# Another order in the passage from a Mamba block to a ternary feed-forward block, and TensorE's loops written out

## The chip, the cores and the metric

The kernel runs on 1 core of a Trainium2 chip. The metric is the device time of one execution in microseconds (us). One execution was also profiled; its rows are the source of all that is read below.

## What is computed

Two sequences of 2048 tokens with 512 features pass one layer. The reference, cut to what matters:

```python
# attention part: a Mamba-2 block (8 heads of 128, state 64, chunks of 64)
zxbcdt = u @ W_in.T
xBC = silu(conv4(xBC) + conv_b);  dt = softplus(dt + dt_bias)
y = ssd(x, dt, -exp(A_log), B, C) + x * D
yg = y * silu(z)
yn = yg * rsqrt(mean(yg * yg) + 1e-5) * norm_w
x1 = layernorm(u + yn @ W_out.T)
# feed-forward part: ternary weights
w_q = clip(round(w / mean|w|), -1, 1) * mean|w|        # for W_up, W_gate, W_down
hidden = silu(x1 @ w_up.T) * (x1 @ w_gate.T)           # 2048 wide
out = layernorm(x1 + hidden @ w_down.T)
```

## The kernel before

The work is cut into 8 blocks of 512 tokens (`NB` = 8, 4 chunks `C` of 128). Each engine runs a program of its own, written out by hand, and they meet through counting semaphores: `wait_ge(sem, n)` holds an engine's whole queue until the count is reached. SyncE (SP) issues all transfers, in its program's order.

*Attention part.* `step(n, par)` does block n in four head pairs p. TensorE projects x and z tiles (`head_tile`, line 931, 12 matmuls of 512 columns each into one of three ring banks), turns x (line 984), makes the states (`states`, line 994) and the outputs (`outputs`, lines 1004 and 1012), and in pair 1 the four output chunks of the block before (`chunk_out`, line 960). VectorE does the convolution (1793), the mask (`within`, which writes `seg`, 1891), the state updates (1905, the last of which writes `carry`), `skip` (1913), and for each chunk `residual` (1928 to 1936) and `normalise` (1940). GpSimd takes the root for `rstd` (1584). The outputs of a block's last head pair come in the next block's pair 0. For each chunk SP loads the token rows (`load_utok`, line 620) once the residual two chunks before is done, and stores the normalised rows (`store_x1`, line 624). `run_steps` calls blocks 0 and 1, then a hardware loop (line 524, two turns of two blocks) for 2 to 5, then 6 and 7.

*Feed-forward part.* `x1` of a block is split into a high and a low half-precision part in seven pieces (j = 0 to 6, factors and sums of a Strassen-like scheme of seven products): ScalarE writes the high part (`x_high`, 1402), VectorE the low (`x_low`, 1968), SP transposes both (`turn_x`, DMA transposes, line 695). Each hidden group q (eight to a block) takes products 1 to 7 (line 1126, 8 matmuls of 256 columns each). Products 1, 6 and 7 go to one bank in turn; ScalarE reads the bank after each (`chain_read`, 1504) into `s1`, `u2` and `u3`, and VectorE adds (`summed`, 2143) to get `c11`, `c12`, `c21`, `c22`. Then come ScalarE's tanh (1513), VectorE's `hidden` (2151), GpSimd's `hidden` (1704), ScalarE's high part (1521), VectorE's `hidden_low` (2158), and TensorE's `down` (1146). `ffn_steps` calls step(-1), 0 and 1, then a hardware loop (line 537, two turns of two steps) for 2 to 5, then 6 and 7. TensorE is one of five engines with these two loops.

*The passage.* Block 7 of the attention part already splits and transposes block 0 for the feed-forward part, in its pairs 1 and 2. After block 7, TensorE does product 1 of (block 0, q = 0), then the last head pair's outputs between the other products. `ffn_step(-1)` (q = 1 to 7) still has to finish block 7's output chunks: `last_squares` (1167) sums the squares, VectorE writes `ms` (2228), GpSimd the root `rms` (1747), `last_chunk(c, half)` (1183) makes the chunks in the two `p_down` banks, and VectorE takes `residual(7, c)` in steps q = 2, 3, 4 and 6. `last_chunk(2, 0)` in step 3 needs the bank of chunk 0 and so waits for `residual(7, 0)`. The function that calls TensorE's blocks in the attention part is

```python
def run_steps(eng, step):
    step(0, 0)
    step(1, 1)
    with eng.Fori(0, QN // 2) as i:
        step(i * 2 + Q0, 0)
        step(i * 2 + (Q0 + 1), 1)
    step(NB - 2, 0)
    step(NB - 1, 1)
```

Of the kernel before, what the change touches and what calls it, by code (L numbers as in the profile page):

```python
# [32 lines left out]
NB = 8  # L33
# [126 lines left out]
def build(nc, a, out):  # L160
    with ExitStack() as ctx:
# [156 lines left out]
        turn_free = sem("turn_free")  # L318
# [260 lines left out]
        def _(sp):  # L579
# [134 lines left out]
            def step(n, par):  # L714
                for p in range(4):
# [24 lines left out]
                    if p == 2:  # L740
                        if not is_at(n, 0):
                            if is_at(n, NB - 1):
                                for j in range(4):
                                    turn_x(0, 0, j)
                            store_x1(n - 1, 0)
                            load_utok(n - 1, 2)
                            if is_at(n, NB - 1):
                                turn_x(0, 0, 4)
                            store_x1(n - 1, 1)
                            load_utok(n - 1, 3)  # L750
                            store_x1(n - 1, 2)
# [132 lines left out]
        def _(pe):  # L884
# [231 lines left out]
            run_steps(pe, step)  # L1116
# [81 lines left out]
            product(0, 0, 0, 1, True)  # L1198
            pe.wait_ge(s1_ok, 1)
            product(0, 0, 0, 6, False)  # L1200
            pe.wait_ge(turn_free, turn_use(NB, "x01") + 1)
            product(0, 0, 0, 5, True)
# [69 lines left out]
            ffn_steps(pe, ffn_step)  # L1272

        @block.scalar
        def _(act):
# [258 lines left out]
            gated(NB, 0, 1)  # L1534
            act.wait_ge(scales_ok, 3)
            gated(NB, 1, 0)
            gated(NB, 1, 1)

            def ffn_step(t, par):
                n, own = t + 1, 1 - par  # L1540
                for q in range(1 if is_at(t, -1) else 0, NQ):
                    before, earlier = pair_at(t, par, q, 1), pair_at(t, par, q, 2)
                    if before:
                        m, its, k = before
                        wait(act, act_ok, 2 * (m * NQ + k) - 1)
# [3 lines left out]
                    if has_up(t):  # L1549
                        wait(act, act_ok, 2 * (n * NQ + q) - 2)  # L1550
                        chain_read(n, q, s1, prod[1], s1_ok, c11_ok)
                    for j in splits_at(t, q):
                        x_high(t + 2, par, j)
                    if before:
                        hidden_tanh(m, k, True, not has_up(t))
                        hidden_tanh(m, k, False, not has_up(t))
# [8 lines left out]
        def _(pool):  # L1565
# [167 lines left out]
            def ffn_step(t, par):  # L1733
                for q in range(1 if is_at(t, -1) else 0, NQ):
# [7 lines left out]
                    if before:  # L1742
                        m, its, k = before
                        hidden(m, k, True)
                        if is_at(t, -1) and q == 2:
                            pool.wait_ge(ms_ok, 1)
                            pool.tensor_tensor(rms[:, :], ms[:, :], exponent[:, :], ALU.pow).then_inc(rms_ok, 1)
                        hidden(m, k, False)
# [8 lines left out]
        def _(dve):  # L1757
# [277 lines left out]
            def step(n, par):  # L2035
                first, end = is_at(n, 0), is_at(n, NB)
                for p in range(2 if first else 0, 4):
# [51 lines left out]
                    if p == 1 and is_at(n, NB - 1):  # L2089
# [6 lines left out]
                        residual(n - 1, 0, ring[ring_bank("chunk", 0)])  # L2096
                        x_low(0, 0, 2)
                        x_low(0, 0, 3)
                        normalise(n - 1, 0)
                        residual(n - 1, 1, ring[ring_bank("chunk", 1)])  # L2100
                        x_sum(2)
                        x_low(0, 0, 4)
                        normalise(n - 1, 1)
                        residual(n - 1, 2, ring[ring_bank("chunk", 2)])
                        x_sum(3)
                        normalise(n - 1, 2)
# [204 lines left out]
```

## Time and profile before

| | |
|---|---|
| time, median of 3 runs | 1399.34 us (1397.88 to 1401.0) |
| the profiled execution's own time | 1399.36 us |
| its span, first to last instruction | 1397.6 us |
| TensorE matmuls busy | 1348.4 us (96%) |
| VectorE busy | 1069.8 us (77%) |
| ScalarE busy | 787.5 us (56%) |
| GpSimd busy | 649.8 us (46%) |
| mean granted TensorE clock | 0.992 |
| mean busy share of the DMA queue q1 | 35.6% |

In the rows PE is TensorE's matmuls and PEld its weight loads, DVE is VectorE, ACT ScalarE, POOL GpSimd, SPq SyncE's queue. `[2.94 <-DVE carry L1905]` says that the engine had been idle for 2.94 us and that VectorE's instruction of line 1905, which writes `carry`, released it; "issue" says that nothing in the profile held it. Ends of matmuls are modelled. Buffers are reused under other names in the feed-forward part: there `ring`, `p_seg` and `p_st` hold the chain of products 1, 6 and 7, `p_turn` products 3 and 5, `cum_g` is `s1` and `u2`, `grow` is `u3`, `xdt` holds `c21` and `c22`, `rows` the token rows and the residual.

### The profile page before, as it was taken

The numbers are of one execution on the slowest core, as the hardware profiler recorded it, in microseconds if no ns is written. First come the engines' busy times: TensorE is split into PE (matmuls) and PEld (weight loads), VectorE is DVE, ScalarE is ACT, GpSimd is POOL, SyncE is SP. The second block draws the span as 40 slices with busy tenths as digits, with TensorE's granted clock in tenths as the row PEclk, the third lists the DMA queues.
The fourth block names the chain that finished last, engine by engine and source line by source line (L and its number), as shares of the span: only waits on it lengthen the run. The fifth ranks groups of instructions, "written<-read, shape, count | busy, mean of one in ns | idle before, by whom it ended". The sixth has DMA issues, their size and how long they took to land.

```text
span 1397.6 us, 27164 instructions
## 1 busy us (share of the span) xinstructions
PE 1348.4 (96%) x9446; PEld 872.8 (62%) x9446; DVE 1069.8 (77%) x1848; ACT 787.5 (56%) x1561; POOL 649.8 (46%) x628
## 2 busy tenths in 40 slices
PE   8899999999999999999989999999999999999998
PEld 4455555555555555555546677777777767777774
DVE  6887887886887878868686777777777767777775
ACT  6686574773855837738556555454454545444441
POOL 0574264573663746625346434344343434444331
PEclk9899999999999999999999999999999999999999
DMA  7436333262443542523647342213232222222102
GB/s 246 158 129 224 128 106 99 84 174 79 106 122 98 152 109 80 160 85 95 158 141 225 69 136 47 83 47 67 59 72 69 71 62 58 80 61 54 31 24 68
DMA packets 162798, 143.87 MB, mean 103 GB/s; under 512 B 101344, under 2 KB 123232, under 8 KB 161504
## 3 DMA queue, kind: packets, MB, share of 16 engines
q1 hardware_dynamic: 162656, 142.05, 35.6%
q8 instruction: 80, 1.31, 0.4%
q14 instruction: 62, 0.51, 0.1%
HBM read 99.93 MB, written 27.39 MB: 91 GB/s over the span
## 4 chain that ended last, share of the span: by engine, by line
PE 55%; issue 14%; DVE 13%; ACT 9%; POOL 6%; DMA 1%; SPq 1%; ACTq 0%; POOLq 0%; DVEq 0%
PE ring L1146 15%; PE p_turn L1126 7%; PE p_y L1126 7%; PE p_st L1126 5%; PE p_seg L1126 5%; PE ring L931 5%; PE ring L960 4%; DVE acc L1793 3%; ACT p_seg L1363 2%; ACT xdt L1354 2%; DVE seg L1891 2%; PE p_y L1004 1%; POOL sq_sum L1621 1%; PE p_y L1012 1%; DVE st L1905 1%
## 5 line engine op out<-in xcount | busy, mean ns | idle before, releaser
L931 PE MATMUL ring<-u_split,weights 128*128 128x512 f16 x1620 | 377.6, 383 | 2.3 <-DVE x_ch L1798 2.0
L931 PEld LDWEIGHTS ring<-u_split,weights 128*128 128x128 f16 x1620 | 155.5, 99 | 173.8 <-issue 9.9
L1704 POOL TENSOR_TENSOR xdt<-xdt 128x512 f32<-128x512 f32 x64 | 100.7, 1573 | 340.9 <-DVE xdt L2151 340.9
L1793 DVE SCALAR_TENSOR_TENSOR acc<-ring,taps,acc 128x511 f32<-128x511 f32 (+2 forms) x192 | 143.7, 749 | 4.5
L960 PE MATMUL ring<-w_out,raw 128*128 128x512 f16 x672 | 147.1, 379 | 0.0
L1354 ACT ACTIVATE xdt<-p_turn,dts 128x128 f32<-128x128 f32 x256 | 73.0, 376 | 73.7 <-PE p_turn L984 73.7
L960 PEld LDWEIGHTS ring<-w_out,raw 128*128 128x128 f16 x672 | 65.8, 99 | 77.7
L1613 POOL TENSOR_TENSOR raw<-yg,raw 128x512 f16<-128x512 f32 x64 | 78.8, 1231 | 76.0 <-ACT raw L1384 75.3
L1608 POOL TENSOR_TENSOR yg<-y_ch,z_ch 128x512 f32<-128x512 f32 x64 | 81.6, 1275 | 46.3 <-DVE y_ch L1913 46.3
L1307 ACT ACTIVATE ring<-acc 128x512 f32<-128x512 f32 x64 | 38.5, 602 | 87.1 <-DVE acc L1793 86.6
L1363 ACT ACTIVATE p_seg<-cum_rows,cum 128x128 f32<-128x128 f32 x256 | 80.8, 388 | 10.1 <-DVE seg L1891 10.1
L1004 PE MATMUL p_y<-seg,xdt 128*128 128x128 f32 x512 | 70.6, 281 | 15.0 <-DVE seg L1891 14.7
L1584 POOL TENSOR_TENSOR rstd<-var_e,exponent 128x1 f32<-128x1 f32 x32 | 20.1, 627 | 130.0 <-DVE var_e L1936 130.0
L1004 PEld LDWEIGHTS p_y<-seg,xdt 128*128 128x128 f32 x512 | 64.3, 191 | 25.3 <-DVE seg L1891 20.9
L1621 POOL TENSOR_TENSOR sq_sum<-sq_sum,sq 128x512 f32<-128x512 f32 x56 | 71.2, 1272 | 0.0
L1513 ACT ACTIVATE cum_g<-c_dec,tanh_scale 128x512 f32<-128x512 f32 x32 | 23.1, 722 | 73.4 <-DVE b_dec L2143 73.4
L1513 ACT ACTIVATE cum_g<-b_dec,tanh_scale 128x512 f32<-128x512 f32 x32 | 23.1, 722 | 71.5 <-DVE c_dec L2143 70.9
L1891 DVE TENSOR_TENSOR seg<-p_seg,cb_mask 128x512 f32<-128x512 f32 x64 | 43.9, 686 | 21.3 <-ACT p_seg L1367 21.3
L1513 ACT ACTIVATE grow<-xdt,tanh_scale 128x512 f32<-128x512 f32 x64 | 45.9, 717 | 19.6 <-DVE xdt L2143 19.0
L1798 DVE SCALAR_TENSOR_TENSOR x_ch<-ring,acc 128x512 f32<-128x512 f32 x64 | 44.1, 689 | 15.0 <-ACT ring L1307 14.0
L2143 DVE TENSOR_TENSOR xdt<-grow,p_turn 128x512 f32<-128x512 f32 x64 | 44.0, 687 | 13.9 <-ACT grow L1504 8.2
L2143 DVE TENSOR_TENSOR c_dec<-cum_g,p_turn 128x512 f32<-128x512 f32 x32 | 22.0, 689 | 39.4 <-PE p_turn L1126 39.4
(392 smaller groups left out, 3306.5 us busy)
## 6 DMA issues: line engine op xcount, KB each, us to landing
cum_rows<-cum_dram SPq DMA_DIRECT2D x64, 256.0 KB, 4.2
quant<-in_w_ffn SPq DMA_DIRECT2D x24, 512.0 KB, 4.4
quant<-in_w_ffn SPq DMA_DIRECT2D x48, 256.0 KB, 4.1
cum_g<-cum_dram SPq DMA_DIRECT2D x64, 128.0 KB, 4.5
rows<-in_u_tok SPq DMA_DIRECT2D x32, 256.0 KB, 4.3
x_dram<-rows SPq DMA_DIRECT2D x32, 256.0 KB, 2.0
tern_ug<-quant SPq DMA_DIRECT2D x32, 256.0 KB, 3.4
u_raw<-in_u_t SPq DMA_DIRECT2D x7, 1024.0 KB, 8.1
```

Source lines behind the costliest of these rows:

```text
L931: mm = pe.matmul(bank_k[:, :], w_in[:, ws, k, col:col + P], us[:, par, k * T:(k + 1) * T], start=(i == 0), stop=(i == 3 * KD - 1))
L960: mm = pe.matmul(ring[b][:, :], ys[:, h, c * P:(c + 1) * P], w_out[:, ws, h, :], start=(h == 0 and ys is y_hi and ws == 0), stop=(h == H - ...
L1004: pe.matmul(p_y[q][:, c * P:(c + 1) * P], xdt[:, q, c, :], seg[:, q, c, :], start=(c == 0), stop=False, skip_group_check=True)
L1126: mm = pe.matmul(bank_j[:, w * 256:(w + 1) * 256], factor(weight, w, k, q), xs[par][i][:, k, :], start=(first and w == 0 and k == 0 and xs ...
L1146: mm = pe.matmul(p_down[c % 2][:, :], hidden_tile(par, m, low)[:, c * P:(c + 1) * P], t_down(m), start=(e == 0 and m == 0 and not low), st ...
L1354: ins = act.activation(xdt[:, q, c, :], p_turn[:, c * P:(c + 1) * P], ACT.Copy, scale=dts[:, owner, c, h:h + 1])
L1363: ins = act.activation(p_seg[:, c * P:(c + 1) * P], cum_b[:, (2 * p - 2 + q) % 4, c, :], ACT.Relu, bias=cum[:, owner, h, c:c + 1], scale=-1.0)
L1513: act.activation(th[second], up, ACT.Tanh, scale=tanh_scale[:, 0:1]).then_inc(tanh_ok, 1)
L1608: pool.tensor_tensor(yg[:, q, :], y_ch[:, q, :], z_ch[:, k % 4, :], ALU.mult).then_inc(yg_ok, 1)
L1621: pool.tensor_tensor(sq_sum[:, :], sq_sum[:, :], sq[:, q, :], ALU.add).then_inc(sqsum_ok, 1)
L1704: pool.tensor_tensor(tile_[:, 1, :, :], tile_[:, 0, :, :], tile_[:, 1, :, :], ALU.mult).then_inc(hid_ok, 1)
L1793: dve.scalar_tensor_tensor(acc[:, buf, k + 1:T], own[:, 0:T - 1 - k], taps[:, h, 2 - k:3 - k], acc[:, buf, k + 1:T], ALU.mult, ALU.add).th ...
```

## The change

The order of steps changes in four engines' programs, in the passage only; and TensorE's two loops are replaced by calls for each block, while the other engines keep theirs.

- SP, block 7: stores and row loads of block 6's chunks come earlier among the transposes.
- TensorE: product 5 of (0, 0) moves ahead of product 6.
- ScalarE: the reads of product 7 of (0, 0) and of product 1 of (0, 1) move ahead of `gated(8, 1, 0)` and `gated(8, 1, 1)`; in `ffn_step(-1)` the first tanh moves ahead of `x_high`.
- GpSimd, step (-1), q = 2: `rms` comes ahead of `hidden`.
- VectorE: in block 7 another order of `residual`, `normalise`, `x_low` and `x_sum`; in `ffn_step(-1)` the first `hidden` ahead of `x_low`, and `residual(7, 0)` ahead of `c12` instead of at the step's end.

```diff
@@ SP, block NB - 1, p == 2
-                                for j in range(4):
+                                for j in range(2):
                                     turn_x(0, 0, j)
                             store_x1(n - 1, 0)
                             load_utok(n - 1, 2)
                             if is_at(n, NB - 1):
-                                turn_x(0, 0, 4)
+                                for j in range(2, 4):
+                                    turn_x(0, 0, j)
                             store_x1(n - 1, 1)
                             load_utok(n - 1, 3)
+                            if is_at(n, NB - 1):
+                                turn_x(0, 0, 4)
                             store_x1(n - 1, 2)
                             store_x1(n - 1, 3)
@@ TensorE
-            run_steps(pe, step)
+            for n in range(NB):
+                step(n, n % 2)
...
             product(0, 0, 0, 1, True)
+            pe.wait_ge(turn_free, turn_use(NB, "x01") + 1)
+            product(0, 0, 0, 5, True)
             pe.wait_ge(s1_ok, 1)
             product(0, 0, 0, 6, False)
-            pe.wait_ge(turn_free, turn_use(NB, "x01") + 1)
-            product(0, 0, 0, 5, True)
...
-            ffn_steps(pe, ffn_step)
+            ffn_step(-1, 1)
+            for t in range(NB):
+                ffn_step(t, t % 2)
@@ ScalarE
             gated(NB, 0, 1)
+            chain_read(0, 0, u3, prod[7], u3_ok, c21_ok)
             act.wait_ge(scales_ok, 3)
             gated(NB, 1, 0)
+            chain_read(0, 1, s1, prod[1], s1_ok, c11_ok)
             gated(NB, 1, 1)
...
+                    if before and not (is_at(t, -1) and q == 1):
                         wait(act, act_ok, 2 * (m * NQ + k) - 1)
                         chain_read(m, k, u3, prod[7], u3_ok, c21_ok)
                     if earlier:
                         hidden_high(*earlier, False)
-                    if has_up(t):
+                    if has_up(t) and not (is_at(t, -1) and q == 1):
                         wait(act, act_ok, 2 * (n * NQ + q) - 2)
                         chain_read(n, q, s1, prod[1], s1_ok, c11_ok)
-                    for j in splits_at(t, q):
-                        x_high(t + 2, par, j)
+                    if not is_at(t, -1):
+                        for j in splits_at(t, q):
+                            x_high(t + 2, par, j)
                     if before:
                         hidden_tanh(m, k, True, not has_up(t))
+                    if is_at(t, -1):
+                        for j in splits_at(t, q):
+                            x_high(t + 2, par, j)
+                    if before:
                         hidden_tanh(m, k, False, not has_up(t))
@@ GpSimd
-                        hidden(m, k, True)
                         if is_at(t, -1) and q == 2:
                             pool.wait_ge(ms_ok, 1)
                             pool.tensor_tensor(rms[:, :], ms[:, :], exponent[:, :], ALU.pow).then_inc(rms_ok, 1)
+                        hidden(m, k, True)
                         hidden(m, k, False)
@@ VectorE, block NB - 1, p == 1
                         residual(n - 1, 0, ring[ring_bank("chunk", 0)])
+                        normalise(n - 1, 0)
+                        residual(n - 1, 1, ring[ring_bank("chunk", 1)])
                         x_low(0, 0, 2)
                         x_low(0, 0, 3)
-                        normalise(n - 1, 0)
-                        residual(n - 1, 1, ring[ring_bank("chunk", 1)])
+                        normalise(n - 1, 1)
                         x_sum(2)
+                        residual(n - 1, 2, ring[ring_bank("chunk", 2)])
                         x_low(0, 0, 4)
-                        normalise(n - 1, 1)
-                        residual(n - 1, 2, ring[ring_bank("chunk", 2)])
+                        normalise(n - 1, 2)
                         x_sum(3)
-                        normalise(n - 1, 2)
                         residual(n - 1, 3, ring[ring_bank("chunk", 3)])
                         normalise(n - 1, 3)
@@ VectorE, feed-forward step
+                    if attention_rest(t, q) == 0:
+                        residual(NB - 1, 0, p_down[0])
                     if before:
                         summed(m, k, "c12", u2, u2_ok, 5, ALU.add)
                     if has_up(t):
                         summed(n, q, "c11", s1, s1_ok, 2, ALU.add)
+                    if is_at(t, -1) and before:
+                        hidden(m, k, True)
                     for j in splits_at(t, q):
                         x_low(t + 2, par, j)
...
                     if before:
-                        hidden(m, k, True)
+                        if not is_at(t, -1):
+                            hidden(m, k, True)
                         hidden(m, k, False)
...
-                    if attention_rest(t, q) is not None:
+                    if attention_rest(t, q):
                         residual(NB - 1, attention_rest(t, q), p_down[attention_rest(t, q) % 2])
```

## Rows read from the trace of the kernel before

**Rows 1.** Busy time by stretches: window, us, engines (instructions), PEclk, DMA, GB/s.

```profile
715.85:719.26 3.41, 3.41 (x10) 1.20 (x9) 3.34 (x6) 2.31 (x6) 2.91 (x4) 0.50 0.30 79
749.00:825.00 76.00, 70.52 (x570) 53.52 (x567) 54.53 (x92) 38.24 (x65) 41.10 (x33) 1.00 0.50 148
825.00:1128.00 303.00, 303.00 (x2282) 223.01 (x2280) 228.70 (x359) 152.45 (x252) 126.21 (x95) 1.00 0.26 66
1128.00:1140.00 12.00, 9.13 (x70) 6.63 (x69) 5.01 (x8) 3.54 (x7) 2.86 (x2) 1.00 0.44 139
```

**Rows 2.** TensorE, 749 to 825 us: start, us, engine, line, operation, idle, releaser.

```profile
751.31 1.05 PE L1126 MATMUL ring<-b_tok,weights 128*128 128x256 f16 x8 [0.69 <-ACT cum_g L1504]
...
756.04 1.05 PE L1126 MATMUL ring<-u_raw,weights 128*128 128x256 f16 x8
...
762.06 1.05 PE L1126 MATMUL p_turn<-c_ch,weights 128*128 128x256 f16 x8 [1.37 <-DVE xdt L2143]
...
781.35 2.76 PE L1183 MATMUL ring<-w_out,raw 128*128 128x512 f16 x12 [1.55 <-DVE rows L1928]
...
819.81 1.05 PE L1126 MATMUL p_turn<-c_ch,cum_rows 128*128 128x256 f16 x8 [1.44 <-DVE xdt L2143]
820.70 1.04 PE L1126 MATMUL p_seg<-b_tok,weights 128*128 128x256 f16 x8
```

**Rows 3.** Timeline of TensorE in block 7.

```profile
714.86 1.09 PE L994 MATMUL p_st<-xdt,b_dec 128*64 128x128 f32 x16 [2.94 <-DVE carry L1905]
715.89 4.42 PE L931 MATMUL ring<-u_split,weights 128*128 128x512 f16 x12
...
721.78 1.16 PE L1004 MATMUL p_y<-seg,xdt 128*128 128x128 f32 x8 [0.58 <-DVE seg L1891]
```

**Rows 4.** Timeline of SyncE's queue and VectorE in block 7.

```profile
703.69 0.43 SPq L620 DMA_DIRECT2D rows<-in_u_tok  x1
...
706.52 0.75 DVE L1928 SCALAR_TENSOR_TENSOR rows<-ring,rms,rows 128x512 f32<-128x512 f32 x1 [2.93 <-DMA rows<-in_u_tok]
...
710.05 0.75 DVE L1928 SCALAR_TENSOR_TENSOR rows<-ring,rms,rows 128x512 f32<-128x512 f32 x1
...
721.04 0.68 DVE L1891 TENSOR_TENSOR seg<-p_seg,cb_mask 128x512 f32<-128x512 f32 x1
```

**Rows 5.** Timeline of ScalarE, VectorE and GpSimd in the passage.

```profile
760.63 0.58 ACT L1504 ACTIVATE grow<-ring 128x512 f32<-128x512 f32 x1
...
771.16 0.15 DVE L2228 TENSOR_SCALAR ms<-ring 128x4 f32<-128x4 f32 x1
...
775.24 0.69 DVE L2143 TENSOR_TENSOR b_dec<-cum_g,p_turn 128x512 f32<-128x512 f32 x1 [3.27 <-PE p_turn L1126]
...
779.42 1.02 POOL L1747 TENSOR_TENSOR rms<-ms,exponent 128x4 f32<-128x4 f32 x1
...
780.54 0.75 DVE L1928 SCALAR_TENSOR_TENSOR rows<-ring,rms,rows 128x512 f32<-128x512 f32 x1 [2.21 <-issue]
...
817.95 0.99 DVE L2158 SCALAR_TENSOR_TENSOR z_ch<-xdt,hid_scale,z_ch 128x512 f16<-128x512 f32 x1
```

**Rows 6.** The loop lines 524 and 537: ns min/median/max, first to last start.

```profile
L524 PEldq COMPARE_BRANCH  x2: 83/2503/4923, 371.6 to 557.5; - x2
...
L537 PEldq COMPARE_BRANCH  x2: 83/1790/3497, 1128.5 to 1284.8; - x2
```

**Rows 7.** Timelines of TensorE and VectorE behind the jumps back of both loops.

```profile
376.81 0.65 PE L984 MATMUL p_turn<-ident,x_ch 128*128 128x128 f32 x4 [1.80 <-issue]
...
379.58 1.41 DVE L1913 SCALAR_TENSOR_TENSOR y_ch<-x_ch,d_skip,p_y 128x512 f32<-128x512 f32 x2 [4.20 <-issue]
...
388.46 1.16 PE L1004 MATMUL p_y<-seg,xdt 128*128 128x128 f32 x8 [0.77 <-DVE seg L1891]
...
1134.18 0.69 DVE L2143 TENSOR_TENSOR xdt<-grow,p_turn 128x512 f32<-128x512 f32 x1 [2.77 <-ACT grow L1504]
...
1137.26 1.04 PE L1126 MATMUL p_turn<-c_ch,cum_rows 128*128 128x256 f16 x8
```

## The prediction

> **What bounds the kernel now.** I read four views: the busy time by stretches, the timelines around the idle spots of TensorE, the list of waits, and the rows of the two loop lines.
>
> The stretches [rows 1] show the bound. In the feed-forward part, 825 to 1128 us, TensorE is busy 303.00 of 303.00 us: nothing that another engine does there costs time, and whatever TensorE gains earlier is kept to the end. From 749 to 825 it is busy 70.52 of 76.00 us, and from 1128 to 1140, around the jump back of the feed-forward loop, 9.13 of 12.00. Those, with the stretch before 725, hold what this change can win or lose. TensorE's shown ends are modelled: a product of eight 256-column matmuls shows 1.05 us, and the next starts 0.89 after it [rows 2]. So a stall costs TensorE the shown idle time plus about 0.17 us (1.05 - 0.89 = 0.16).
>
> **Part 1, the row loads and the vector order of block 7 (before 725 us).** `states(7, 2)` stands 2.94 us behind VectorE's carry update; the matmuls after it then take 4.42 us for a tile whose like takes 2.76 [rows 2, 3], since TensorE is granted 0.50 of its clock from 715.85 to 719.26 [rows 1]; and the second half of `outputs` waits 0.58 more for `seg` [rows 3]. What VectorE does before: `residual(6, 2)` waits 2.93 us for its token rows, whose load is issued at 703.69 behind four transposes, and `residual(6, 3)` starts at 710.05, its load issued after residual 2; the second `seg` of block 7 follows at 721.04 [rows 4].
>
> The diff issues store 0 and load 2 after two transposed splits instead of four. Both need only residual 0 and normalise 0, which on VectorE now come before splits 2 and 3. Load 3 takes the place at 703.69 that load 2 had. Then residual 2 is limited by TensorE's chunk, not by a load, and residual 3 can start when rows issued at 703.69 land: 706.52 by the row of today's load 2. That is 710.05 - 706.52 = 3.53 us earlier. What is left between residual 3 and the second `seg` (710.05 to 721.04) keeps its order, so `seg` ends 3.5 us earlier and so does TensorE's wait on it. The 2.94 stall goes: the carry that released `states` at 714.86 is then there at 711.3, and TensorE comes to it at 714.86 - 2.94 = 711.92. The half clock goes with it. In exchange the wait before the second half of `outputs` grows from 0.58 to about 1.5 us, so not all of 2.94 + (4.42 - 2.76) + 0.58 = 5.2 comes back. I take **3.5**. Bounds: 0 if a transpose lands later because a load is now ahead of it and splits 2 to 4 stand before residual 3 as late as today, 5.2 if VectorE also gets shorter.
>
> **Part 2, TensorE and ScalarE at the start of the feed-forward part.** Product 6 waits 0.69 us for ScalarE's read of product 1 [rows 2]. Product 5, whose only wait is for ScalarE's `x_dt`, the same that `states` asked for before it, is put between: 0.89 us of work covers 0.69 + 0.17. **0.9**, bounds 0.7 and 0.9.
>
> Product 3 of step q = 1 waits 1.37 us for `c22`, which waits for ScalarE's read of product 7 at 760.63 [rows 2, 5]. That read stands behind two `gated` groups that wait for GpSimd, though product 7 starts at 756.04 and ends near 757. The diff puts it ahead of them: the read then ends near 757, `c22` and `c21` follow `c11` on VectorE near 758 to 759, and TensorE comes to product 3 at 759.6 in the new time. The read of product 1 of q = 1 moves up too, between the two `gated`; it asks for a product that ends at about 759, when the second `gated` would start anyway. **1.5** (1.37 + 0.17). Lower bound 0.5: the next thing TensorE asks for is the last `y_low` of GpSimd, now due within 0.2 us of the time when TensorE comes to it, so a microsecond may come back as a wait there.
>
> **Part 3, the residual of the last block and `rms`.** `last_chunk(2, 0)` waits 1.55 us for residual 0 at 780.54, which waits for `rms`. `ms` is written at 771.16 but GpSimd makes `rms` at 779.42, behind the `hidden` of the same step [rows 2, 5]. The diff makes `rms` first, so it is there near 772.3 in today's time, and puts the residual before `c12` on VectorE, in an idle stretch of 3.27 us. Its four short instructions should end by 774.5; `c12` starts only at 775.24, when product 3 is done [rows 5], so nothing is pushed. **1.7** (1.55 + 0.17), bounds 0.7 (if `c12` is pushed and product 5 waits) and 1.7.
>
> The earlier `hidden` in the splits' steps lets GpSimd start 0.6 us sooner per step. Only at q = 7 does TensorE wait there: 1.44 us for `c22` behind `hidden_low` at 817.95 [rows 2, 5]. VectorE is contiguous before it: `c11`, split, `hidden`, `hidden`, residual 3, `hidden_low`, and the sum stays the same in any order. I take **0.1**, bounds 0 and 1.6. The moved `x_high` and splits have microseconds of slack, since their transposes feed products that come later: 0.
>
> **Part 4, the loops of TensorE.** The rows of the two loop lines hold two branches each on TensorE: 83 ns where it falls through, 4923 and 3497 ns where it jumps back [rows 6]. After the jumps TensorE shows idle 1.80 us and 12.00 - 9.13 = 2.87 us [rows 1, 7]; its queued matmuls cover the rest. Written out, those jumps are gone. But VectorE, ScalarE, GpSimd and SyncE keep theirs.
>
> Feed-forward jump: TensorE would reach product 3 at 1137.26 - 2.87 - 2 x 0.17 = 1134.05. That product needs `c22`, which VectorE starts at 1134.18 after its own jump and ends at 1134.87 [rows 7]. TensorE waits 0.9 there. 3.2 - 0.9 = **2.3**; bounds 1.5 and 3.2 (if VectorE's jump too gets shorter once TensorE's fetch is gone).
>
> Attention jump: VectorE is idle 4.20 us until 379.58, and then works without a gap up to the `seg` that TensorE waits for before 388.46 (0.77 us) [rows 7]. If TensorE comes 1.80 us earlier it waits that much longer at 388.46. **0**; bounds 0 and 2.0, the latter if VectorE's own 4.20 shrinks.
>
> **A rule against the trace.** The rows say 4923 and 3497 ns for the two jumps back and 83 ns for falling through [rows 6]. The Trainium skill, Advanced Engine Details and Errata, section Control Flow Timing, gives about 108 ns for a compare-and-branch. By that figure, four branches cost 0.4 us and part 4 would be worth nothing that can be measured; the sum by it would be 1391.7. This trace does not agree with it for a jump that is taken. The skill's page Runtime: NRT & Kernel Launch, Instruction fetch mechanics, says instead that a taken branch out of the fetched window forces a fetch before execution can go on, which is the side the rows are on.
>
> **The sum.** 3.5 + 0.9 + 1.5 + 1.7 + 0.1 + 2.3 + 0 = 10.0 us. The profiled execution took 1399.36 us with a span of 1397.6, so 1.8 us lie around the span; the median of the three runs shown is 1399.34, the same. 1399.4 - 10.0 = **1389.4 us**, 0.7% less.
>
> **Rivals.**
> - *The fetch stalls of the other engines shrink too.* After TensorE's jump VectorE stalls 4.20 us, longer than the feed-forward jump's 2.77 [rows 7]; if TensorE's fetch was in its way, the attention jump gives up to 2.0 and the feed-forward jump 0.9 more: 1386.5 us. Against it: no row shows that the two stalls have a common cause, and VectorE's jump stays. 0.15.
> - *Part of the stalls turns into new waits* (the `y_low` of part 2, a split behind a later transpose in part 1, or the jumps give nothing because the idle time comes from elsewhere, 10.0 - 2.3). Gains of 3 to 8 us, centre 1393. 0.16.
> - *No effect*: the gaps are taken up by VectorE, whose work is unchanged. It is the releaser in most rows of [rows 2, 3]. For it to hold, part 1 must give nothing and parts 2 and 3 must return at q = 7, where TensorE waits for VectorE. Within 2.8 us of before: 1398. 0.04.
> - *Slower: the written-out stream is fed late.* The loops' turns are 557.5 - 371.6 = 186 and 1284.8 - 1128.5 = 156 us long [rows 6], so 684 us are written out. If a refill comes late it costs what the jump cost, 3.5 to 4.9 us [rows 6]; from the third late refill on, 3 x 4.9 = 14.7 outweighs 10.0 and the kernel gets slower: about 1404 us. Against it: 825 to 1128 runs straight ahead, without a jump back, and shows no such idle in 303 us [rows 1]. 0.04.
> - The forecast as it stands, 8 to 12 us gained: 0.61.
>
> **Numbers.** Prediction 1389.4; its own case spans 1387.4 to 1391.4. The range takes in the first rival and most of the second: 1386.0 to 1394.5. About 0.2% (2.8 us) is what a measurement of this kernel can tell from no change. Faster 0.92, same 0.04, slower 0.04.
>
> **What would show it.** Part 1: no idle before `states` at block 7's third head pair, no half clock near 715, load 3 issued before transposed split 4, the wait before the second `outputs` half at about 1.5 us. Part 2: product 5 between 1 and 6; no wait of product 3 at q = 1. Part 3: `rms` about 1 us after `ms`, `last_chunk(2, 0)` without idle; the wait at q = 7 still there. Part 4: no idle of TensorE right at the two former jumps, but longer waits on `seg` (2.5 instead of 0.77) and of about 0.7 on `c22` behind it; VectorE's own idle there unchanged. The prediction is wrong if residual 3 does not start some 3.5 us sooner relative to block 7, if the last `y_low` holds TensorE for more than 1 us, or if the other engines' jumps change length.

## The result and the profile after

The changed kernel takes 1388.67 us (median of 5 runs, 1387.74 to 1391.2) against 1398.60 for the kernel before (5 runs on the same chip, 1396.11 to 1401.0): ratio 0.9935, 95% interval 0.9921 to 0.9949, or 9.9 us less by the medians. The profiled execution took 1387.94 us with a span of 1386.2. The forecast was 1389.4.

Where the time came from is read in the same way for every run below: the start of the same matmul is compared in two traces. TensorE's first matmul is set to zero in both, and the difference is how far the stream has come ahead of the kernel before. Taken at twelve matmuls it gives the gain of each stage (us, minus is earlier). Each row is one profiled execution:

| kernel | start to 374 | attention jump | to 710 | block 7 | prod. 6 | prod. 3, q=1 | `y_low` | `last_chunk(2,0)` | q=4 | q=7 | 825 to 1128 | feed-forward jump |
|---|---|---|---|---|---|---|---|---|---|---|---|---|
| changed kernel | -2.19 | -0.53 | -0.08 | -4.14 | -0.87 | -1.54 | +0.30 | -1.72 | +0.61 | +0.63 | 0.00 | -1.87 |
| e1_order_only | -1.37 | -1.10 | -0.13 | -3.18 | -0.86 | -1.54 | +0.31 | -1.72 | +0.61 | +0.63 | 0.00 | -0.58 |
| e2_loops_only | -1.87 | -0.64 | -0.15 | -1.03 | 0.00 | 0.00 | 0.00 | 0.00 | -0.01 | +0.02 | 0.00 | -2.08 |
| e3_hidden_last | +0.16 | -1.11 | -0.15 | -4.14 | -0.87 | -1.54 | +0.31 | -1.72 | 0.00 | 0.00 | 0.00 | -2.05 |
| e4_all_straight | -1.97 | -2.56 | -1.32 | -4.14 | -0.86 | -1.54 | +0.31 | -1.72 | +0.61 | +0.63 | +1.41 | -3.21 |
| e5_block7_only | -2.38 | -1.05 | -0.18 | -3.31 | -0.01 | 0.00 | 0.00 | 0.00 | -0.01 | -0.01 | 0.00 | +0.27 |
| e6_block7_vector | -1.45 | -0.09 | +0.01 | +4.19 | 0.00 | +0.01 | 0.00 | 0.00 | -0.01 | 0.00 | 0.00 | +0.43 |
| e8_best | -1.36 | -2.57 | -1.43 | -4.15 | -0.87 | -1.54 | +0.31 | -1.72 | 0.00 | 0.00 | 0.00 | -3.21 |
| e9_residual_later | -1.36 | -2.56 | -1.33 | -4.14 | -0.86 | -1.54 | +0.31 | -1.72 | -0.01 | +0.05 | +0.75 | -3.21 |
| e10_reads_back | +0.15 | +0.08 | -0.08 | -4.14 | -0.87 | +0.37 | 0.00 | -1.72 | +0.61 | +0.93 | +1.10 | -2.10 |
| e11_rms_back | -0.44 | -0.93 | -0.11 | -4.15 | -0.86 | -1.54 | +0.30 | -0.16 | +0.61 | +0.62 | 0.00 | -2.05 |
| e12_fetch_on | -0.40 | -0.94 | -0.07 | -3.60 | -0.86 | -1.54 | +0.32 | -1.72 | +0.61 | +0.96 | +1.07 | -2.10 |
| e13_fetch_off | -0.33 | -0.40 | +0.03 | -1.88 | -0.87 | -1.54 | +0.31 | -1.72 | +0.61 | +0.62 | 0.00 | -2.28 |

The first column moves by up to 2.5 us between kernels whose code there is the same, so it is the chance of one execution; the second does by 1.2. From product 6 to q = 7 equal code gives equal numbers to some 0.02 us, but for two cases told below: e10 and e12, where lower clock begins in the column q = 7, and block 7, where TensorE's instruction packets play a part. The feed-forward jump is less exact: kernels that keep the loop there show -0.58, +0.27 and +0.43. Without the first column the changed kernel has 9.2 us, which agrees with the times within their interval.

The passage in the changed kernel, TensorE's timeline (the rows that answer to [rows 2, 3]):

```profile
709.03 1.09 PE L997 MATMUL p_st<-xdt,b_dec 128*64 128x128 f32 x16
710.06 2.76 PE L934 MATMUL ring<-u_split,weights 128*128 128x512 f16 x12
...
714.82 1.16 PE L1007 MATMUL p_y<-seg,xdt 128*128 128x128 f32 x8 [1.11 <-DVE seg L1905]
...
779.51 2.75 PE L1187 MATMUL ring<-w_out,raw 128*128 128x512 f16 x12
...
783.67 1.05 PE L1130 MATMUL p_turn<-c_ch,weights 128*128 128x256 f16 x8 [0.53 <-DVE xdt L2157]
...
810.26 1.05 PE L1130 MATMUL p_turn<-c_ch,cum_rows 128*128 128x256 f16 x8 [2.06 <-DVE xdt L2157]
...
1125.84 1.05 PE L1130 MATMUL p_turn<-c_ch,cum_rows 128*128 128x256 f16 x8 [1.17 <-DVE xdt L2157]
```

`states` has no wait, its next tile takes 2.76 again, the wait on the second `seg` grew from 0.58 to 1.11, and the waits of [rows 2] are gone save the last, which went from 1.44 to 2.06. New is 0.53 at q = 4 (with 0.17 more at the product behind it, not shown). Busy time by stretches, those of [rows 1] in the new time (window, us, engines with instructions, PEclk, DMA, GB/s):

```profile
711.71:715.12 3.41, 2.30 (x16) 1.65 (x14) 3.27 (x10) 3.30 (x6) 1.62 (x3) 1.00 0.56 175
741.50:815.47 73.97, 70.73 (x575) 54.13 (x575) 60.59 (x92) 39.27 (x67) 42.43 (x32) 1.00 0.51 155
815.47:1118.46 302.99, 302.99 (x2282) 223.00 (x2280) 229.41 (x359) 151.87 (x252) 126.14 (x95) 1.00 0.26 66
1118.46:1129.50 11.04, 9.88 (x74) 7.04 (x73) 5.71 (x9) 4.45 (x8) 3.38 (x3) 1.00 0.50 147
```

VectorE is busy 60.59 us in the passage, where it was 54.53 [rows 1], with the same 92 instructions. That is the lead to the new wait.

### The profile page after: what moved, and what is told of

Its sections match the earlier page's. It is cut to its first block, busy times and chain, and to the rows that moved or that the text cites. A ratio compares the mean times of both kernels' runs of the same rounds, so it can differ in the third digit from the quotient of the medians.

```text
span 1386.2 us, 26970 instructions
## 1 busy us (share of the span) xinstructions
PE 1344.7 (97%) x9446; PEld 872.4 (63%) x9446; DVE 1075.3 (78%) x1848; ACT 786.7 (57%) x1561; POOL 650.7 (47%) x628
## 3 DMA queue, kind: packets, MB, share of 16 engines
q8 instruction: 75, 1.23, 0.4%
## 4 chain that ended last, share of the span: by engine, by line
PE 44%; issue 22%; DVE 14%; POOL 9%; ACT 9%; DMA 1%; POOLq 0%; ACTq 0%; SPq 0%; DVEq 0%
PE ring L1150 11%; PE p_turn L1130 5%; PE p_y L1130 5%; PE ring L934 5%; PE ring L963 5%; PE p_st L1130 4%; PE p_seg L1130 4%; DVE acc L1807 3%; ACT p_seg L1369 3%; ACT xdt L1360 2%; DVE seg L1905 1%; PE p_y L1007 1%; POOL sq_sum L1635 1%; PE p_y L1015 1%; DVE st L1919 1%
```

## The experiments

Times are medians. Each ratio is against the kernel before as it was measured beside them on the same chip: 1397.87 us for e1 to e4, 1397.84 for e5, e6, e8 and e9, 1397.55 for e10 and e11, 1397.79 for e12 and e13. Beside the changed kernel it was 1398.60, so a difference of 1 us between the median of a run and the 1388.67 of the changed kernel shows nothing by itself; small terms are read from the table.

### Which half does it: the order or the loops

**e1_order_only** is the changed kernel with TensorE's loops kept, **e2_loops_only** the kernel before with only them written out.

```diff
e1:  -            for n in range(NB):
     -                step(n, n % 2)
     +            run_steps(pe, step)
e2:  the reverse, in the kernel before
     (both also for ffn_steps)
```

> The changed kernel with TensorE's two loops put back: only the order of steps in the passage differs from before. If the parts add up as the two traces read (order 9.9 us up to the end of the wait at q = 7 less the losses there, jumps 2.5), this gains about 6.7 us over before, so 1391.9 against 1398.6, and TensorE shows idle 1.80 us behind the attention jump and 2.87 in the stretch of the feed-forward jump again. Rival: the straight code also helps in the passage (a refill that came late there), then the order alone gains under 5 us.

> The kernel before with TensorE's two loops written out and nothing else changed. Theory, that the jump's stall on TensorE goes and the wait for VectorE's own jump takes part of its place: gain 2.5 us (0.6 in the attention part, 1.9 in the feed-forward part), TensorE idle about 1.2 us at each of the two places, and VectorE's idle behind the attention jump 2.8 us instead of 4.2. Rival, that a compare-and-branch costs some 0.1 us and the idle time comes from elsewhere: no gain. Rival, that VectorE's shorter stall in the attention part was chance: gain 1.9, VectorE idle 4.2 again.

e1: 1393.92 us (12 runs), ratio 0.9976 (0.9963 to 0.999). e2: 1395.53 (11 runs), 0.9977 (0.9965 to 0.999). In the table the two halves add up in block 7 and the passage to the changed kernel: block 7 3.18 + 1.03 = 4.21 against 4.14. But 1.03 us of block 7 comes from the loops, though TensorE's code there is the same. By the times e1's theory (6.7 us) failed: its median is 4.0 us under the kernel before, 3.4 by the ratio, where its trace has 5.8 from block 7 to q = 7. The two medians together give 6.3 us of the 9.9. The traced execution of e1 took 1390.45 us, and its runs go from 1389.82 (mean granted clock 0.996) to 1400.59 (0.991): the four at 0.991 took 1395.96 to 1400.59, the two at 0.995 and 0.996 1392.29 and 1389.82. So part of the gap goes with the clock. Why e1 is at the lower clock more often is not explained.

### The new waits at q = 4 and q = 7

**e3_hidden_last**: the changed kernel with VectorE's first `hidden` and ScalarE's first tanh back behind the splits.

```diff
-                    if is_at(t, -1) and before:
-                        hidden(m, k, True)
                     for j in splits_at(t, q):
                         x_low(t + 2, par, j)
...
                     if before:
-                        if not is_at(t, -1):
-                            hidden(m, k, True)
+                        hidden(m, k, True)
                         hidden(m, k, False)
     (on ScalarE x_high stands ahead of the first tanh again)
```

> The changed kernel with one part undone: in the steps -1, VectorE's first hidden stands behind the splits again, and ScalarE's first tanh behind its split. Theory: GpSimd's hidden product, started sooner, runs beside VectorE's splits and its normalise and stretches them (2.36 us for two splits instead of 1.28), which gave TensorE 0.53 us of wait at q = 4 and 2.06 instead of 1.44 at q = 7. Then the split pair takes 1.28 us again, the wait at q = 4 is under 0.1, that at q = 7 about 1.4, and the kernel is 1.2 us faster than the changed one. Rival: the residuals that come earlier, not the hidden, load VectorE; then both waits stay and the time too.

1387.56 us, ratio 0.9923 (0.991 to 0.9936). The wait at q = 4 is gone and the one at q = 7 is 1.44 again: 1.24 us by the trace. The medians are 1.1 us apart, and the intervals of the two ratios overlap, so it is the trace that shows the size. The mechanism stands in the timelines of the changed kernel, VectorE and then GpSimd:

```profile
776.32 0.69 DVE L2165 SCALAR_TENSOR_TENSOR xdt<-grow,xdt 128x512 f32<-128x512 f32 x1
776.92 2.36 DVE L1982 TENSOR_TENSOR u_raw<-quant,u_raw 128x512 f16<-128x512 f32 x2
...
786.58 0.69 DVE L1982 TENSOR_TENSOR u_raw<-quant,u_raw 128x512 f16<-128x512 f32 x1
787.19 1.50 DVE L1954 TENSOR_SCALAR rows<-rows,mv,rstd 128x512 f32<-128x512 f32 x1
...
805.17 1.76 DVE L2165 SCALAR_TENSOR_TENSOR b_dec<-cum_g,b_dec 128x512 f32<-128x512 f32 x1
```

```profile
777.08 1.65 POOL L1718 TENSOR_TENSOR xdt<-xdt 128x512 f32<-128x512 f32 x1 [1.52 <-DVE xdt L2165]
...
786.75 1.65 POOL L1718 TENSOR_TENSOR xdt<-xdt 128x512 f32<-128x512 f32 x1 [3.56 <-DVE xdt L2165]
...
804.73 1.65 POOL L1718 TENSOR_TENSOR xdt<-xdt 128x512 f32<-128x512 f32 x1 [2.66 <-DVE xdt L2165]
```

The early `hidden` lets GpSimd start in the middle of VectorE's splits. In this trace an instruction of VectorE with both inputs in SBUF that starts while GpSimd's runs ends only behind it: 804.73 + 1.65 = 806.38, and VectorE's `hidden`, 0.69 alone, ends at 806.93. Of the instructions with one SBUF input only `normalise` is held, at 1.50 instead of 0.54; the statistics of 789.98, beside GpSimd's of 789.36, take their 0.69. It works the other way too: from the passage on GpSimd's `hidden` takes 1.65 to 1.71 us in all 52 cases where it starts inside such an instruction of VectorE, and 1.27 in nearly all of the other 76. In e3 the two splits are done before GpSimd starts, and take 1.29:

```profile
778.01 1.29 DVE L1977 TENSOR_TENSOR u_raw<-quant,u_raw 128x512 f16<-128x512 f32 x2
779.22 0.54 DVE L1949 TENSOR_SCALAR rows<-rows,mv,rstd 128x512 f32<-128x512 f32 x1
779.67 0.68 DVE L2160 SCALAR_TENSOR_TENSOR xdt<-grow,xdt 128x512 f32<-128x512 f32 x1
780.28 0.69 DVE L2160 SCALAR_TENSOR_TENSOR c_dec<-cum_g,c_dec 128x512 f32<-128x512 f32 x1
780.88 0.75 DVE L1937 SCALAR_TENSOR_TENSOR rows<-ring,rms,rows 128x512 f32<-128x512 f32 x1
```

The `hidden` of 780.28 began ahead of GpSimd's at 780.44 and was not held; the residual of 780.88, which reads `ring` in PSUM, was not either. The Trainium skill, SBUF — State Buffer, section "SBUF: two separate sides", says that VectorE (with two SBUF inputs, or in a two-port mode) and GpSimd share one pair of ports, that it is an exclusive lock, and that whoever starts first keeps it for the whole instruction. The trace agrees: VectorE lost 0.96 to 1.08 us each time in the rows above.

### What the other engines' loops cost

**e4_all_straight**: the changed kernel with the loops of all five engines written out.

```diff
 def run_steps(eng, step):
-            step(0, 0)
-            step(1, 1)
-            with eng.Fori(0, QN // 2) as i:
-                step(i * 2 + Q0, 0)
-                step(i * 2 + (Q0 + 1), 1)
-            step(NB - 2, 0)
-            step(NB - 1, 1)
+            for n in range(NB):
+                step(n, n % 2)
     (the same in ffn_steps; two conditions that knew the loop's blocks by
      their type now go by the block's number)
```

> The changed kernel with the loops of all five engines written out, not only TensorE's. Theory: what is left at the two jumps are the jumps of VectorE and ScalarE. Then TensorE's 1.23 us idle at 375.8 and 1.17 at 1124.6 go, each with about 0.17 more, and VectorE's idle of 2.8 and 3.2 us there too: 2.5 to 3 us faster than the changed kernel. Rival: more code for five engines means more refills on the shared queues, some of them late: no gain, or idle spots at new places.

1384.92 us, ratio 0.9907 (0.9893 to 0.992). The attention jump now gives 2.56 us and the feed-forward jump 3.21, with no idle time of TensorE behind either; 1.24 us more come before 710, where TensorE's waits on `seg` from 392 us on sum to 4.0 us instead of 5.0. Against that, 1.41 us are lost behind the wait at q = 7. Stretches of e4 behind that wait, same columns as above:

```profile
807.40:809.20 1.80, 1.80 (x16) 1.48 (x15) 1.80 (x4) 0.72 (x1) 0.00 (x0) 0.83 1.01 378
809.20:812.40 3.20, 3.20 (x19) 2.29 (x18) 3.14 (x4) 1.78 (x3) 1.50 (x1) 0.56 0.41 154
```

The granted clock falls towards its lower level (1.2 GHz) after the 2.06 us of idle time. The changed kernel has the same 2.06 and stays at 1.00. Of seven profiles with that wait, three (e4, e10, e12) show the fall, at 1.40 us each (in e10 and e12 0.3 of it stands in the column q = 7 of the table); of the seven where it is at most 1.50, none shows a fall there.

### Block 7: the row loads, the vector order, and what neither did

**e5_block7_only** is the kernel before with the block 7 edits of SP and VectorE, **e6_block7_vector** with VectorE's alone.

```diff
e5 and e6, VectorE, block 7:
                         residual(n - 1, 0, ring[ring_bank("chunk", 0)])
+                        normalise(n - 1, 0)
+                        residual(n - 1, 1, ring[ring_bank("chunk", 1)])
                         x_low(0, 0, 2)
                         x_low(0, 0, 3)
     ...
e5 alone, SP:
-                                for j in range(4):
+                                for j in range(2):
                                     turn_x(0, 0, j)
     ...
```

> The kernel before with the order of block 7 alone (the row load of block 3 issued ahead of the transposing load on SP, residual 2 and 3 moved on VectorE), every loop as before. Theory: TensorE's stream comes ahead by 2.9 to 3.2 us in block 7 (the loops-only run, which has none of it, already came ahead 1.0 us there, so about 1 us of the 4.1 us seen is not this edit's), so the time falls by about 3 us, ratio 0.998. Rival: the gain of block 7 is the transposes' pace of one execution; then the time stays within 1 us of before.

> The same, but with VectorE's order alone; SP issues its loads as before. If the seg wait of block 7 was VectorE standing behind residual 2 for its row load (2.93 us), the order on VectorE alone removes it: as much gain as with both edits (about 3 us) as long as the rows of block 3 still land before they are read. If the row load is what counts, residual 3 now waits for it, and less than 1.5 us is gained.

e5: 1394.80 us (12 runs), ratio 0.9981 (0.997 to 0.9993), block 7 3.31 us earlier. e6: 1401.83 (12 runs), 1.0028 (1.0015 to 1.0041), slower. The theory (3 us gained) was wrong; its alternative had the mechanism, residual 3 waiting for its load, but not the loss. VectorE, e6:

```profile
705.12 0.75 DVE L1928 SCALAR_TENSOR_TENSOR rows<-ring,rms,rows 128x512 f32<-128x512 f32 x1 [6.17 <-DMA rows<-in_u_tok]
...
712.70 0.75 DVE L1928 SCALAR_TENSOR_TENSOR rows<-ring,rms,rows 128x512 f32<-128x512 f32 x1 [3.52 <-DMA rows<-in_u_tok]
```

With the loads where they were, residual 2 waits 6.17 us, now with the split of j = 4 behind it, whose transpose stands on SP ahead of the load of residual 3 (issued at 709.49, before it was 707.34); residual 3 waits 3.52 more, and TensorE 7.13 for the carry. The vector order is worth something only with the loads. Whether the loads alone would do it was not run.

In e1 and e5, with the loops kept, residual 3 waits 1.99 and 1.94 us for its rows; in the changed kernel they are there (landed at 702.68) and it waits 1.12 for TensorE's chunk. VectorE, e5, then changed kernel:

```profile
703.12 0.75 DVE L1931 SCALAR_TENSOR_TENSOR rows<-ring,rms,rows 128x512 f32<-128x512 f32 x1 [1.94 <-DMA rows<-in_u_tok]
```

```profile
703.09 0.75 DVE L1942 SCALAR_TENSOR_TENSOR rows<-ring,rms,rows 128x512 f32<-128x512 f32 x1 [1.12 <-PE ring L963]
```

With the shift of the stream taken out (3.61 and 2.81 us), residual 3 starts 3.32 us sooner in e5 and 4.15 in the changed kernel, and block 7 gives 3.31 and 4.14: its start sets the gain of block 7.

The 1.03 us of e2 in block 7 has another source. In the four traces with TensorE's loops kept, four transposes of block 7 take 6.44 to 6.66 us on SP's queue; in the eight of e1 to e11 and the changed kernel with them written out, 5.45 to 5.55. Kernel before, then changed kernel, each in the window of those four transposes (DMA queues: packets, MB, share):

```profile
689.38 6.50 SPq L695 DMA_TRANSPOSE xs_more<-u_raw  x4
...
q1 hardware_dynamic: 1766, 1.54, 115.0%
q8 instruction: 1, 0.02, 0.8%
```

```profile
686.56 5.46 SPq L695 DMA_TRANSPOSE xs_more<-u_raw  x4
...
q1 hardware_dynamic: 1855, 1.57, 103.5%
```

A 16 KB packet of instructions (0.88 us long, at 693.41) falls among them before and not after. There are 80 of them before and 75 after, and 75 still in e4 and e8, where the other engines' loops are written out too: so they are TensorE's. Two runs move them on purpose. **e12_fetch_on** and **e13_fetch_off** make eight and four head tiles of block 2 of twice as many, half as wide matmuls:

```diff
-                        mm = pe.matmul(bank_k[:, :], w_in[:, ws, k, col:col + P], us[:, par, k * T:(k + 1) * T], ...)
+                        for at in range(0, T, T // parts):
+                            mm = pe.matmul(bank_k[:, at:at + T // parts], w_in[:, ws, k, col:col + P],
+                                           us[:, par, k * T + at:k * T + at + T // parts], ...)
...
+    parts = 2 if is_at(n, 2) and kind == "x" and h < 8 else 1      (h < 4 in e13)
```

In these two the second half's first matmul restarts the bank, so part of the sums of the split tiles is dropped and the results are not those of the layer; everything else is as in the changed kernel.

> The changed kernel, with the twelve 512-column matmuls of each of eight head tiles of block 2 made as twice as many 256-column matmuls: 96 more matmuls with 96 more weight loads, whose columns are the same in number. TensorE's instruction stream gets 192 instructions longer far ahead of block 7, so each later 16 KB piece of it is fetched some 19 us earlier in the program: the one at 709.1 us comes near 690, within the four transposes of block 7 (686.56 to 692.02), as it did in the kernel before (693.4, within 689.38 to 695.88). Theory: the packet of about 1 us holds up the transposes, which take 6.4 to 6.7 us again instead of 5.5, and TensorE's stream gains 3.2 us in block 7 instead of 4.1: about 1 us slower than the changed kernel. Rival: where the fetch falls has nothing to do with it; 5.5 us and 4.1 us stay.

> The same with four head tiles of block 2 split, 96 instructions more. The fetch comes near 699 us, outside the four transposes. Theory: they stay at 5.5 us and block 7 keeps its 4.1 us; the time is that of the changed kernel plus what the 48 added matmuls cost by themselves (nothing, if two of 256 columns take as long as one of 512). Rival (any split of the tiles slows block 7): 6.5 us here as well.

e12: 1390.50 us, ratio 0.9946 (0.9927 to 0.9965). The packet starts at 687.80 (1.74 us long) and the first transpose takes 2.63 us instead of 1.5; the four take 6.54 us, and block 7 gives 3.60 instead of 4.14:

```profile
687.98 6.54 SPq L695 DMA_TRANSPOSE xs_more<-u_raw  x4
```

e13: 1392.48 us, 0.9956 (0.9943 to 0.997). The four stay at 5.50, but the packet, at 698.46, meets the next pair of transposes, which takes 3.36 us (2.57 in the changed kernel, and in the kernel before):

```profile
698.75 3.36 SPq L695 DMA_TRANSPOSE u_raw<-u_raw  x2
...
q8 instruction: 1, 0.02, 2.1%
```

TensorE's wait on `seg` becomes 1.82, its mean granted clock 0.84 and 0.82 in the two stretches from 715 to 725, and block 7 gives 1.88 instead of 4.14 us. Of the 2.26 lost 0.71 is the longer wait; the rest comes with the lower clock, and e1, e2 and e5 with waits of 1.94 to 2.24 at the same place keep the full clock. So e13 missed its aim as a control, but shows a second collision at another place. In all six block 7 traces with a packet beside a transpose, that one transpose takes 0.7 to 1.2 us longer than its like; in the eight without, none does. The packet is not all of it: in the kernel before and in e6 the packet adds 0.66 us, and the first of the four takes 1.93 and 1.78 instead of 1.41 to 1.55 with no packet near; why is open. The price on TensorE was 0.54 us in e12 and 0.8 to 1.0 by e1 and e5 against the changed kernel, not always the expected 1.

### The smaller terms by themselves

**e10_reads_back** puts ScalarE's two early reads back, **e11_rms_back** GpSimd's `rms` and VectorE's residual 0.

```diff
e10:
-            chain_read(0, 0, u3, prod[7], u3_ok, c21_ok)
             act.wait_ge(scales_ok, 3)
             gated(NB, 1, 0)
-            chain_read(0, 1, s1, prod[1], s1_ok, c11_ok)
             gated(NB, 1, 1)
     (and the two reads of q = 1 stand in ffn_step(-1) again)
e11:
+                        hidden(m, k, True)
                         if is_at(t, -1) and q == 2:
                             pool.wait_ge(ms_ok, 1)
                             pool.tensor_tensor(rms[:, :], ms[:, :], exponent[:, :], ALU.pow).then_inc(rms_ok, 1)
-                        hidden(m, k, True)
     (and on VectorE residual(NB - 1, 0) stands at the step's end again)
```

> The changed kernel with ScalarE's two early chain reads (product 7 of one step, product 1 of the next) back behind the two gated groups. Theory: product 3 of q=1 waits 1.37 us for c22 again, the small wait on the last y_low (0.30 us) goes, so TensorE loses 1.2 us net and the time rises from 1388.7 to about 1389.9. Rival: the wait's microsecond comes back from the later waits (q=4, q=7), then no change. The profile's TensorE shift decides, the time alone can't tell 1.2 us well.

> The changed kernel with GpSimd's rms behind hidden and residual 0 behind c12, as before. Theory: last_chunk(2, 0) waits 1.55 us again, so 1.7 us are lost: 1390.4. Rival: since the first hidden of each step now stands ahead of the splits on VectorE, GpSimd comes to rms sooner than before and less than 1 us is lost.

e10: 1392.18 us, ratio 0.9955 (0.9943 to 0.9968), 3.5 us above the changed kernel. Product 3 waits 1.74 us, 1.91 more lost, and the 0.30 of `y_low` comes back. Of the rest 1.40 is the second effect of above: the wait at q = 7 is followed by lower clock here (0.30 + 1.10). e11: 1390.96, 0.9953 (0.9941 to 0.9965), `last_chunk(2, 0)` waits 1.39: 1.56 us lost, as the theory said.

### The best of it

**e8_best** is e4 with the order of e3; **e9_residual_later** adds, at q = 6 and 7, the first `hidden` ahead of the split, and moves the last residual and its `normalise` to q = 7.

```diff
e9, VectorE, on top of e8 (in its order of execution):
+                    if is_at(t, -1) and q >= 6:
+                        hidden(m, k, True)
                     for j in splits_at(t, q):
                         x_low(t + 2, par, j)
+                    if is_at(t, -1) and q == 7:
+                        residual(NB - 1, 3, p_down[1])
+                        hidden(m, k, False)
+                        normalise(NB - 1, 3)
     (GpSimd's root for this chunk moves to q = 7 with them)
```

> The changed kernel with the loops of all five engines written out and the first hidden values of a step (and the tanh behind them) back behind the splits. Theory: from the all-engines run (1384.9) the new wait at q=4 (0.6 us) and the longer wait at q=7 (0.6 us) go, and with the shorter wait also the stretch of half clock behind it (1.4 us): 1382.3, between 1381.5 and 1384. Rival: the half clock comes whatever the wait's length, then 1383.7; or the two stalls add less together, 1384.9.

> The previous kernel with, at q=6 and q=7 of the passage, the first hidden value ahead of the split, and the last residual and its normalise moved from q=6 to q=7 behind the chunk's last elementwise step. Theory: the TensorE wait of 1.44 us at q=7 is VectorE's queue ahead of the hidden value it needs; with 1 us of it moved behind, the wait falls to about 0.4 and the time to about 1381.3. Rival: the normalised rows are then late for the transposes of the feed-forward part and the wait reappears there: 1382.3 to 1384.

e8: 1381.95 us, ratio 0.9882 (0.9864 to 0.99), the fastest measured here, 6.7 us under the changed kernel, as expected (1382.3). e9: 1383.58, 0.99 (0.9883 to 0.9917). The intervals of the two overlap; by the traces e9 loses 0.8 us against e8. Its wait at q = 7 is 1.50 still. VectorE's `hidden_low` for it starts earlier, but beside GpSimd's next `hidden`, and takes 1.65 instead of 0.99; the `hidden` of VectorE ahead of it was held too (1.75). VectorE, then GpSimd, e9:

```profile
804.11 1.65 DVE L2159 SCALAR_TENSOR_TENSOR z_ch<-xdt,hid_scale,z_ch 128x512 f16<-128x512 f32 x1 [0.24 <-ACT z_ch L1517]
```

```profile
803.94 1.27 POOL L1703 TENSOR_TENSOR b_dec<-b_dec 128x512 f32<-128x512 f32 x1 [0.63 <-DVE b_dec L2152]
```

And the next product waits 0.58, behind the residual and `normalise` moved there.

## Why the prediction held, and where it did not

The total was right (1389.4 for 1388.67), in part by luck. In the trace some terms gave 2.0 us less than the sum had (the earlier `hidden` 1.3, the feed-forward jump and the returned `y_low` 0.7), and two gave 1.2 more (block 7 0.6, the attention jump 0.5).

- **Part 1, 3.5.** Its own edits give 3.2 to 3.3 (e1, e5). With them alone the mechanism went as told: load 3 in front of the last transpose, residual 3 waiting for it (1.99 and 1.94 us), no half clock; the wait on `seg` was 2.07 and 1.94 us where 1.5 was written. In the changed kernel the loops' share came on top, and with it residual 3 waited for TensorE's chunk (1.12 us) instead of the load, which the prediction had for residual 2 alone, and the wait on `seg` was 1.11.
- **Part 2, 0.9 and 1.5.** 0.87 and 1.54, with 0.30 returned by the last `y_low`, the term that its lower bound named.
- **Part 3, 1.7.** 1.72; e11 returned 1.56 of it.
- **Part 3, the earlier `hidden`, 0.1 (0 to 1.6).** This failed: it cost 1.24 us, outside its bounds. The step was "the sum stays the same in any order". It counted VectorE's instructions and durations but not that GpSimd, released earlier, runs beside them and lengthens them.
- **Part 4, feed-forward jump 2.3.** 1.87 here, 2.05 to 2.28 in six other traces, against -0.58 to +0.43 where the loop is kept. The wait on `c22` was 1.17 where 0.9 was expected. The upper bound 3.2 is what e4 measured (3.21).
- **Part 4, attention jump 0.** 0.53 in this trace, but kernels with TensorE's loop kept show 0.09 to 1.10 there, and those with it written out -0.08 to 1.11: nothing can be told from 0. The wait had another place than told: not 2.5 us on `seg` (0.56 here, 0.77 before), but 1.23 on ScalarE, which stood 3.00 us behind its own jump; the prediction had looked at VectorE's alone. The upper bound was 2.0; without the other engines' jumps 2.56. TensorE in the changed kernel:

```profile
377.07 0.63 PE L987 MATMUL p_turn<-ident,x_ch 128*128 128x128 f32 x4 [1.23 <-ACT xdt L1360]
```

- **Not in the sum: 0.8 to 1.0 us in block 7** once the loops are written out, of which the place of an instruction packet is the part that e12 and e13 show.

One sign of being wrong was met to the letter, "if the other engines' jumps change length". It was a poor sign, since that length varies with equal code. Of the rivals, "other engines' fetch stalls shrink" has nothing for it: VectorE still stands 2.83 and 3.23 us behind the jumps [rows 7 had 4.20 and 2.77], and the first number is 2.42 to 4.10 in e1, e5 and e6 too. "Part of the stalls turns into new waits" happened, at a size of 0.30 + 1.24 us. The feed of a written-out stream (the slower rival) showed no late refill on TensorE: from 70 us on it has no idle time over 1 us that nothing in the profile explains, in the changed kernel, e4 or e8. The compare-and-branch price of about 108 ns of the Trainium skill (Advanced Engine Details and Errata, Control Flow Timing) is not what a taken jump costs here. Writing the jumps out gave 2 us for TensorE alone and 5.8 us (2.56 + 3.21) for all five engines.

## What to carry to other kernels

Before an instruction of GpSimd is released earlier, look at what VectorE runs at that time: the order that keeps both apart is worth more than the earlier start. A reordering of loads and of the compute behind them is one edit; half of it can be slower than none. A loop written out on the engine that sets the time pays here only as far as the engines that feed it have no jump of their own at the same place.

## What was not expected of the hardware

- One 16 KB packet of TensorE's instructions beside a DMA transpose makes that transpose 0.7 to 1.2 us longer on SP's queue (1.26 to 1.92, 2.06, 2.42 and 2.49; 1.5 to 2.63). Two changes that touch no transpose moved it (e12, e13).
- The same idle time of 2.06 us before the same matmul was followed by a lower clock in three of seven profiles. In block 7 it fell after 1.82 us in e13 and not after 1.94 to 2.24 in e1, e2 and e5. What decides it stays open.
- VectorE's held instruction ends 0.3 to 0.55 us after GpSimd's, and GpSimd's `hidden` takes 1.65 instead of 1.27 us when VectorE's with two SBUF inputs came first.
- The stall behind the attention loop's jump on VectorE, with equal code, was between 2.42 and 4.20 us.
